# Selective scan in units of one state and both channel halves (896 columns instead of 448)

## The reference

```python
u = silu(causal_conv(u)); z = ...                        # (32, 56, 256)
dt = clip(softplus(...), 0.001, 0.1)
b = tanh(u @ b_proj_w + b_proj_b)                        # (32, 56, 16)
c = tanh(u @ c_proj_w + c_proj_b)
a = -exp(a_log)                                          # (256, 16)
da = exp(dt[..., None] * a)
db = (dt * u)[..., None] * b[:, :, None, :]
h = da_t * h + db_t                                      # scan over the 56 steps, h starts at 0
y = einsum('bds,bs->bd', h, c_t)
y = (y + u * d) * silu(z)
x = layernorm(x + residual + y @ out_proj_w + out_proj_b)
```

## Time and profile before

| | us |
|---|---|
| runs shown | 1257.64 (median), 1234.75, 1258.11 |
| the profiled execution | 1235.67 |
| its span | 1233.9 |
| scan loop (L2186 to L2330), from 854.5 to 1056 us of the span | 201.5 |

### The profile page before, as it was taken

The page is one execution under the profiler, slowest core; times in us unless marked ns, Lnnn a source line. Parts: engine busy times, 40 slices in busy tenths (PEclk is TensorE's granted clock), DMA queues, the critical chain, the costliest instruction groups (busy, mean ns, idle before and its releaser), DMA issues. The chain is left out here.

```text
span 1233.9 us, 22903 instructions
## 1 busy us (share of the span) xinstructions
PE 1025.5 (83%) x8317; PEld 747.9 (61%) x8317; DVE 993.4 (81%) x1983; ACT 719.5 (58%) x1522; POOL 594.7 (48%) x899
## 2 busy tenths in 40 slices
PE   5889997476699999999999698690888888768696
PEld 3555653164699999999998566530333333536555
DVE  5989999746699988898886537679999999567575
ACT  3677774055466666666664163275777777147453
POOL 4300000012898888888884141101799999225260
PEclk9899998788899999999999889695899999879989
DMA  3000000020311112111200010002000000000001
GB/s 74 1 1 2 1 2 1 1 107 6 135 51 66 66 74 76 69 67 69 76 2 1 1 24 2 0 1 66 1 0 1 0 1 1 1 1 3 2 1 31
DMA packets 18769, 33.41 MB, mean 27 GB/s; under 512 B 5200, under 2 KB 13888, under 8 KB 18656
## 3 DMA queue, kind: packets, MB, share of 16 engines
q1 hardware_dynamic: 16768, 30.89, 7.3%
q10 hardware_dynamic: 1888, 1.05, 0.4%
HBM read 31.02 MB, written 0.92 MB: 26 GB/s over the span
## 5 line engine op out<-in xcount | busy, mean ns | idle before, releaser
L2256 POOL TENSOR_TENSOR m_h_in<-m_dtu,m_bs 128x448 f32<-128x448 f32 x128 | 144.5, 1148 | 70.4 <-DVE m_dtu L2300 53.6
L774 DVE SCALAR_TENSOR_TENSOR l0r_u<-l0r_u,l0r_a_col 128x1024 f32<-128x1024 f32 x110 | 135.9, 1276 | 6.0 <-ACT l0r_u L684 6.0
L2323 DVE TENSOR_TENSOR_SCAN m_hs<-msp_da,m_h_in 128x448 f32<-128x448 f32 x128 | 136.2, 1081 | 2.4 <-ACT msp_da L2283 1.7
L1155 POOL TENSOR_TENSOR bl_sc<-bl_sc,bl_topall 125x1456 f32<-125x1456 f32 x32 | 105.3, 3290 | 58.3 <-ACT bl_topall L1317 58.3
L684 ACT ACTIVATE l0r_u<-l0r_pu 128x512 f32<-128x512 f32 x216 | 108.4, 642 | 32.3 <-PE l0r_pu L586 32.1
L2219 PE MATMUL msp_py<-m_hc,ident 128*128 128x448 f32 x256 | 118.2, 546 | 0.0
L586 PE MATMUL l0r_pu<-l0r_xs,l0r_eb 32*128 32x256 f32 x896 | 106.4, 460 | 6.9 <-ACT l0r_u L684 4.6
L1392 PE MATMUL bl_pS<-b_qw,bl_xcT 128*125 128x112 f32 x768 | 104.0, 278 | 0.0
L867 POOL MEMSET bq_lT<- 128x256 f32 x1 | 0.3, 312 | 206.6 <-POOLq L108 206.6
L586 PEld LDWEIGHTS l0r_pu<-l0r_xs,l0r_eb 32*128 32x128 f32 x896 | 73.0, 210 | 39.5 <-ACT l0r_u L684 29.0
L2274 ACT ACTIVATE m_bs<-msp_pb 128x448 f32<-128x448 f32 x128 | 69.3, 542 | 45.0 <-PE msp_pb L2203 43.5
(11 more groups left out here) (392 smaller groups left out, 2541.5 us busy)
## 6 DMA issues: line engine op xcount, KB each, us to landing
b_xc<-in_ctx SPq DMA_DIRECT2D x16, 750.0 KB
bl_more<-in_ctx SPq DMA_DIRECT2D x16, 750.0 KB
x_tm<-in_x SPq DMA_DIRECT2D x1, 896.0 KB, 6.6
cw_cT<-in_ctx_headT SPq DMA_DIRECT2D x1, 896.0 KB
out_dram<-x_tm SPq DMA_DIRECT2D x4, 224.0 KB, 2.5
l0r_xr<-in_x ACTq DMA_DIRECT2D x4, 192.0 KB, 5.6
w_up<-in_L_ffn_w SPq DMA_DIRECT2D x1, 512.0 KB, 4.1
w_down<-in_L_ffn_w SPq DMA_DIRECT2D x1, 512.0 KB, 5.3
```

The lines of the kernel that those rows point to most:

```text
L774: ve.scalar_tensor_tensor(state(c, i, r), prev, a_col[:, :], state(c, i, r), ALU.mult, ALU.add).then_inc(s["step"], 1)
L1155: pool.tensor_tensor(sc[0:KP, n % 3, :, :], sc[0:KP, n % 3, :, :], over(topall[0:KP, n % 2, :].unsqueeze(1), [KP, KT + 1, QR]), ALU.subtra ...
L2256: pool.tensor_tensor(h_in[:, n % NU, :], dtu[:, half, cols], bs[:, n % NU, :], ALU.mult).then_inc(s["db"], 1)
L2323: ve.tensor_tensor_scan(hs[:, n % NU, :], da[:, n % 2, 0:CH], h_in[:, n % NU, :], 0.0, ALU.mult, ALU.add).then_inc(s["scan"], 1)
```

## The change

A unit is now one chunk and one state with both halves, 896 columns, so there are 64 units. h_in, hs and hc hold both halves, with NU = 4 buffers. The wide rows of b and c are made once for both halves and read twice by a broadcast (both_halves). pb and pc have one buffer each instead of two; da has two buffers of 1024 columns, and the two halves' decays are still two instructions of ScalarE. TensorE adds each half with an instruction of its own, and both sums of a chunk are in py. GpSimd owns the states 2, 6, 10 and 13. VectorE makes the step product of the first chunk only; those of the other chunks are made by GpSimd in the chunk before (state 7). The step product is no longer negated, and skip subtracts instead. The last gate is shared by VectorE and GpSimd.

```diff
-        NU = 6
-        h_in = sb("h_in", [P, NU, CH])
...
+        NU = 4
+        h_in = sb("h_in", [P, NU, H2, CH])
+        hs = sb("hs", [P, NU, H2, CH])
+        hc = sb("hc", [P, NU, H2, CH])
...
-        UNITS = NC * H2 * DS
+        UNITS = NC * DS
...
-        OWN, AHEAD = (3, 8, 13), 3
+        OWN, AHEAD = (2, 6, 10, 13), NU - 1
...
+        def both_halves(row):
+            return over(row.unsqueeze(1), [P, H2, CH])
...
-            pb, pc = psum2("pb", [P, 2, 512]), psum2("pc", [P, 2, 512])
-            da = psum2("da", [P, 2, 512])
-            py = psum2("py", [P, 2, 512])
+            pb, pc = psum2("pb", [P, 512]), psum2("pc", [P, 512])
+            da = psum2("da", [P, 2, 1024])
+            py = psum2("py", [P, H2, 512])
...
                 def wide_b(n):
...
-                    if n >= 2:
-                        pe.wait_ge(s["bcopied"], n - 1)
...
+                    if n:
+                        pe.wait_ge(s["bcopied"], n)
...
                 def wide_c(n):
...
-                    if n >= 2:
-                        row_read(pe, n - 2)
...
+                    if n:
+                        row_read(pe, n - 1)
...
                 def add(n):
...
-                    pe.matmul(py[:, g % 2, 0:CH], core.ident[:, :], hc[:, n % NU, :], start=(st == 0),
-                              stop=(st == DS - 1)).then_inc(s["summed"], 1)
+                    if st == 0 and k:
+                        pe.wait_ge(s["out"], H2 * k)
+                    for half in range(H2):
+                        last = pe.matmul(py[:, half, 0:CH], core.ident[:, :], hc[:, n % NU, half, :], start=(st == 0),
+                                         stop=(st == DS - 1))
+                    last.then_inc(s["summed"], 1)
...
             @block.gpsimd
...
+                    pool.tensor_tensor(h_in[:, n % NU, :, :], dtu[:, :, span(k)], both_halves(bs[:, n % NU, :]),
                                        ALU.mult).then_inc(s["db"], 1)
                     if n - AHEAD in owned:
                         readout(n - AHEAD)
...
+                    if st == 7 and k + 1 < NC:
+                        pool.tensor_tensor(dtu[:, :, span(k + 1)], dt[:, :, span(k + 1)], u[:, :, span(k + 1)],
+                                           ALU.mult).then_inc(s["dtu"], 1)
+                    if st == 11 and k:
+                        gated(k - 1)
...
-                gated(UNITS // DS - 1)
+                pool.wait_ge(s["out"], H2 * (NC - 1) + 1)
+                pool.tensor_tensor(gT[:, 0, span(NC - 1)], gT[:, 0, span(NC - 1)], sz[:, 0, span(NC - 1)], ALU.mult)
 
             @block.scalar
...
+                    for half in range(H2):
+                        act.activation(da[:, n % 2, half * CH:(half + 1) * CH].rearrange("p (b t) -> p b t", t=L)[:, :, 1:L],
+                                       dt[:, half, span(k)].rearrange("p (b t) -> p b t", t=L)[:, :, 1:L],
+                                       ACT.Exp, scale=alog[:, half, st:st + 1]).then_inc(s["decay"], 1)
                     if n + 2 < UNITS:
                         copy_b(n + 2)
                     if n in owned:
                         act.wait_ge(s["widec"], n + 1)
...
             @block.vector
...
+                ve.tensor_tensor(dtu[:, :, span(0)], dt[:, :, span(0)], u[:, :, span(0)], ALU.mult).then_inc(s["dtu"], 1)
...
+                    ve.tensor_tensor(hc[:, n % NU, :, :], hs[:, n % NU, :, :], both_halves(pc[:, 0:CH]),
+                                     ALU.mult).then_inc(s["hc"], 1)
...
                 for n in range(UNITS):
...
+                    ve.wait_ge(s["decay"], H2 * (n + 1))
                     ve.wait_ge(s["db"], n + 1)
...
+                    ve.tensor_tensor_scan(hs[:, n % NU, :, :].rearrange("p h q -> p (h q)"), da[:, n % 2, 0:H2 * CH],
+                                          h_in[:, n % NU, :, :].rearrange("p h q -> p (h q)"), 0.0, ALU.mult, ALU.add).then_inc(s["scan"], 1)
                     if n and n - 1 not in owned:
                         readout(n - 1)
-                    if n % DS == 3 and n >= DS:
-                        skip(n // DS - 1)
+                    if st == 4 and k:
+                        skip(k - 1)
                 readout(UNITS - 1)
...
+                skip(NC - 1)
+                ve.wait_ge(s["out"], H2 * NC)
+                ve.tensor_tensor(gT[:, 1, span(NC - 1)], gT[:, 1, span(NC - 1)], sz[:, 1, span(NC - 1)], ALU.mult)
```

More of the change, by code:

```diff
@@ L2234, in _, with gated @@
             def _(pool):
[L2235 to L2239, removed]
+                def gated(k):
+                    pool.wait_ge(s["out"], H2 * (k + 1))
+                    pool.tensor_tensor(gT[:, :, span(k)], gT[:, :, span(k)], sz[:, :, span(k)], ALU.mult)
                 def readout(n):
@@ L2246, in readout @@
                         pool.wait_ge(s["summed"], n - NU + 1)
-                    pool.tensor_tensor(hc[:, n % NU, :], hs[:, n % NU, :], cs[:, by_pool(n) % 2, :], ALU.mult).then_inc(s["hc_pool"], 1)
+                    pool.tensor_tensor(hc[:, n % NU, :, :], hs[:, n % NU, :, :], both_halves(cs[:, by_pool(n) % 2, :]),
+                                       ALU.mult).then_inc(s["hc_pool"], 1)
                 for n in range(UNITS):
-                    _, half, _, cols = unit(n)
-                    if n % DS == 0:
-                        pool.wait_ge(s["dtu"], n // DS + 1)
+                    k, st = n // DS, n % DS
+                    if st == 0:
+                        pool.wait_ge(s["dtu"], k + 1)
                     pool.wait_ge(s["bcopied"], n + 1)
@@ L2291, in _ @@
                             act.wait_ge(s["hc_pool"], by_pool(n) - 2)
-                        act.activation(cs[:, by_pool(n) % 2, :], pc[:, n % 2, 0:CH], ACT.Copy).then_inc(s["ccopied"], 1)
+                        act.activation(cs[:, by_pool(n) % 2, :], pc[:, 0:CH], ACT.Copy).then_inc(s["ccopied"], 1)
             @block.vector
             def _(ve):
[L2297 to L2301, removed]
+                ve.memset(da[:, :, 0:H2 * CH:L], 0.0).then_inc(s["zeroed"], 1)
+                ve.tensor_tensor(dtu[:, :, span(0)], dt[:, :, span(0)], u[:, :, span(0)], ALU.mult).then_inc(s["dtu"], 1)
                 def readout(n):
@@ L2308, in readout, with skip @@
                         ve.wait_ge(s["summed"], n - NU + 1)
[L2309 to L2316, removed]
+                    ve.tensor_tensor(hc[:, n % NU, :, :], hs[:, n % NU, :, :], both_halves(pc[:, 0:CH]),
+                                     ALU.mult).then_inc(s["hc"], 1)
+                def skip(k):
+                    ve.wait_ge(s["summed"], (k + 1) * DS)
+                    for half in range(H2):
+                        ve.scalar_tensor_tensor(gT[:, half, span(k)], u[:, half, span(k)], col[:, half, SKIP:SKIP + 1],
+                                                py[:, half, 0:CH], ALU.mult, ALU.subtract).then_inc(s["out"], 1)
                 for n in range(UNITS):
-                    ve.wait_ge(s["decay"], n + 1)
+                    k, st = n // DS, n % DS
+                    ve.wait_ge(s["decay"], H2 * (n + 1))
                     ve.wait_ge(s["db"], n + 1)
```

25 lines of the change are left out of this document (6 added, 19 removed).

## The result

| | before, us | after, us |
|---|---|---|
| runs, median (lowest, highest) | 1249.34 (1234.75, 1258.11) | 1285.99 (1285.36, 1286.54) |
| profiled execution | 1235.67 | 1285.36 |
| its span | 1233.9 | 1283.6 |
| its last gate of the loop ends at | 1055.73 | 1101.94 |

The changed kernel is slower: the ratio of comparable runs is 1.0383, 95% interval 1.0345 to 1.0422. The two runs of before near 1258 are disturbed executions, and the ratios in this document leave such runs out where the medians do not. The profiled executions differ by 49.7 us; 46.2 of that lie before the end of the last gate and 3.5 behind it.

The account below looks back on a forecast made before the run. VectorE's nearly gapless instruction stream was taken as the bound. Savings, 35.0 us of gaps and 3.5 of TensorE order put the last gate at 1082.4, 26.7 later: 1262.4; plus 40 for the clock, 1302, range 1255 to 1345.

Parts of the forecast that it names:

- The cheaper stream: Scan loop: both halves in one instruction, scan 1.95 us, readout 1.00, GpSimd product 2.10; first scan at 858.06 instead of 862.66.
- The end from readout 62: Loop end: last additions one after another, two skips and the shared gate take 10.35 us after readout 62.
- The gap at owned units: Single C row: the next scan waits for row, copy and decays; 2.19 us at each of 16 owned units, 35.0 us.
- Rival D: No gap at owned units and TensorE's additions in time, so only the savings stay: 1223.9 us; chance 0.16.
- The order on TensorE: Addition queued behind the wide C row delays about 29 readouts by 0.12 us each, 3.5 us.
- The clock: TensorE falls to half clock after 3.1 us pauses in most of 16 owned turns; half of 80 taken, 40 us.
- A: The forecast case: gaps at owned units and the clock falling in most turns, 1302 us (1280 to 1330); chance 0.58.
- B: Same gaps at owned units, but TensorE's clock stays up: 1262 us; chance 0.14.
- GpSimd as the bound: GpSimd setting the loop's pace would need 2.4 us per instruction, above twice today's; given no chance of its own.

Follow-up runs that it names:

- e4: The kernel before, with the wide C row of a unit waiting for the readout of n-1 instead of n-2: 1307.44 us, ratio 1.0547 to before.
- e3: The kernel after, with ScalarE's copy of an owned unit's C row issued one decay later: 1277.76 us, ratio 1.029 to before.
- e9: e6 with 12 readouts on GpSimd instead of 16, NU = 6, and skip behind scan 3 of a chunk instead of 4: 1229.65 us, ratio 0.9935 to before.
- e1: The kernel after, with TensorE issuing the ready addition of unit n-3 ahead of the wide C row: 1266.6 us, ratio 1.0194 to before.
- e2: The kernel after, with NU = 6 buffers instead of 4, GpSimd still three ahead: 1284.68 us, ratio 1.0335 to before.
- e7: The kernel after, with three additions of zeros on TensorE in 12 of its 16 pauses: 1281.67 us, ratio 1.0341 to before.
- e11: e1 with skip one state earlier, behind scan 3 of a chunk instead of scan 4: 1259.83 us, ratio 1.0182 to before.
- e6: The kernel after with addition first, B row copied one unit ahead, C row copied two units behind, NU = 5: 1239.86 us, ratio 1.0014 to before.
- e10: The kernel after, with GpSimd owning states 2 and 10 only, 8 units instead of 16: 1279.94 us, ratio 1.0341 to before.

## Why the prediction was right, and where its sizes were wrong

1285.99 lies inside the range of 1255 to 1345 and on the side that had 0.78. Against the profiled execution, 66.7 us more were forecast and 49.7 came. The steps:

- **The cheaper stream: right.** 1.93 in the stream against 1.95 for a scan, 0.98 against 1.00 for a readout, 2.08 against 2.10 on GpSimd. The first scan started at 858.36, forecast 858.06. The end from readout 62 (1091.61) to the last gate (1101.94) was 10.33, forecast 10.35.
- **The gap at owned units: right in place, number and size.** 16 waits of 2.10 or 2.11, the first and the last 2.29, 34.1 us together; the prediction has 2.10 for the wait and 35.0 with the overlap. e4 shows by itself that the single row makes such waits (1.55 in it), e3 moves the gap, e9 removes it.
- **Rival D (no gap): wrong for this order, and near what is possible.** It gave 1223.9; e9, without the gaps, ran at 1229.65.
- **The order on TensorE: a term mis-sized by a missing chain.** The step says that after the readout's end the addition takes until 1.97 and costs 0.12 a readout, 3.5 in all. It stops at the readout. One instruction further stand the row of B, ScalarE's copy and the decays, 3.80 us after the readout's end, and the next scan waits for them. The prediction has that chain only with the clock low ("a scan waits 1.4 more"). With the clock up a turn of four took 13.82 instead of 7.80 + 3.00 + 2.19 + 0.24 = 13.23, of five 16.97 instead of 16.30, of three 10.17 as forecast 10.16: with eight turns of four and three of five 6.7 us more than forecast. e1 and e2 show that it is this chain and not the buffers.
- **The clock: right that it falls, too large.** The term was 40 us, half of 80. TensorE did wait 3.09 us in an owned unit's turn (forecast 3.1), but the clock fell in 7 of 16 turns, not in most. In ordinary turns this cost 6.3 us (e7), in the first turn, which ran at the half clock, 1.8, behind the loop 3.5. The three turns with a skip took 4.4 more than the skip and their units explain; how much of that is the clock and how much the skip's order stays open, since e11, with the skip earlier, was run on e1. So the clock cost 12 to 16 us in all, if all 3.5 behind the loop are its doing, which their size suggests and no run shows by itself. Of the 19.5 by which the last gate lies behind the forecast of 1082.4 with the clock up, 6.7 + 6.3 + 4.4 + 1.8 = 19.2 are told.
- **The likeliest case:** A, with gaps and falls, was the right one, but its 40 was about three times too large while 6.7 were missing; 1286 lies nearly midway between A and B. That 1302 came within 17 us is so in part two errors that offset each other, and the range had room for them because it was 90 us wide.
- **GpSimd: right for after, and closer than thought.** "GpSimd as the bound would need 2.4 us per instruction" holds for the long loop of after. At e6's length it is full in the crowded places, and scans wait 6.3 us for it.
- **Small slips:** the 94.5 us of the earlier trace rows are idle time of TensorE's weight loads (PEld); its products of the row of C waited 31.8 us in the same 100 waits. Half of B's 0.14 is 0.07 for each side, where the sums have 0.08 and 0.06. Nothing in the forecast hangs on these.
- **Left over:** which pauses bring a fall and which don't is not settled by any run.

## What to carry to other kernels

Going from two PSUM buffers to one is priced by following what each in-order engine has queued behind the instruction that now waits, not only the consumer of the buffer: here the way led over TensorE, ScalarE's copy of C, the decays and back to VectorE, and a second time over the addition and the row of B queued behind the row of C. Put what is ready (the addition) ahead of what must wait (the row), and a copy that is not needed at once behind the work that is. A saving in instructions shows only when these orders fit and the load of the helper engine has been counted again for the shorter loop.

## What the runs showed of the hardware

TensorE's clock was less regular than expected. In the turn shown above the pause of 3.09 us ended at 889.10 and the additions behind it took 1.67 us, at 2.4 GHz (granted clock 1.00 from 886 to 891). A pause of the same kind and length later in after had a fall: the additions behind it took 3.19, at 1.2 GHz (0.50 from 945.5 to 950). Its rows in the timeline of TensorE:

```profile
946.37 0.55 PE L2210 MATMUL msp_pc<-m_bc,selector 128*128 128x448 bf16 x1 [3.08 <-DVE m_hc L2312]
946.72 3.19 PE L2219 MATMUL msp_py<-m_hc,ident 128*128 128x448 f32 x4
```

The Trainium skill, TensorE: Matmul & The Clock Gate, "HAM oscillation — how this bites in real kernels", describes a loop in which TensorE waits about 3 to 5 us for a transfer in every turn and the clock falls in every turn. The trace agrees that the falls come with the pauses (e7 filled twelve, and none of those turns was slowed), but with 3.08 or 3.09 us only 7 of 16 turns had one here. Shorter pauses brought some too: nine of e1's falls stood at a pause of 2.47 to 2.87 us, the four of e4 at one of 1.95 to 2.03, and there again not every such pause had one. A fall is also not a price by itself: e1 had 12 of them, 5 more than after, and was 19 us faster, which fits that its readouts waited 5.8 us for TensorE instead of 14.3.

Behind the loop TensorE is the busiest engine, 136.0 us of 178.2 in before, so the clock can matter more there. The output product of after, and of before:

```profile
1102.62 1.06 PE L2341 MATMUL mn_y<-mw_wout,m_gT 128*112 128x128 f32 x4
```

```profile
1057.66 0.60 PE L2334 MATMUL mn_y<-mw_wout,m_gT 128*112 128x128 f32 x4
```

Ahead of it TensorE had stood idle for 2.71 us in after and 2.26 in before; from the last gate to the end took 181.7 us at a granted clock of 0.86 instead of 178.2 at 0.88. Those are the 3.5 us behind the loop; e6 had 181.5 us at 0.86, a like loss. In e10 the same idle time of 2.71 brought no fall at that place, and the part behind the loop took 178.3 us at 0.88. So the time there goes with the clock, and the idle time alone doesn't decide the fall.
